# A decoder layer on one core: the turns of x1 and x2 of 13 groups in 32x32 blocks on VectorE and through DRAM, and another order of a round's products

## The reference

```python
x = _layernorm(x + attn(x))            # linear attention: q (k^T v), no softmax
x = _layernorm(x + xattn(x, ctx, mask))# 16 heads of 32, 154 keys, softmax, masked
x = _layernorm(x + ffn(x))             # r = sigmoid(xr Wr); k = relu(xk Wk)^2; out = r * (k Wv)
# xr, xk: mixes of each row with the row before it (mu_r, mu_k)
```

## Time and profile before

| | |
|---|---|
| median of 3 runs | 916.45 us (916.25 to 916.95) |
| the profiled execution | 914.96 us, its span 912.9 us |
| granted TensorE clock | 0.998 of full speed |
| busy share of the span | PE 98%, PEld 82%, DVE 76%, ACT 61%, POOL 57% |
| moved by DMA | 46.54 MB, mean 51 GB/s |

### The profile page before, as it was taken

How to read it: one execution, slowest core, us unless ns; L and a number is a source line. 1 busy time by engine, 2 the same in 40 slices (tenths; PEclk the granted TensorE clock), 3 DMA queues, 4 the chain that set the end, 5 groups by cost and what they waited for, 6 DMA issues and landing times.

```text
span 912.9 us, 23290 instructions
## 1 busy us (share of the span) xinstructions
PE 896.7 (98%) x8774; PEld 749.0 (82%) x8774; DVE 695.6 (76%) x1994; ACT 556.5 (61%) x1667; POOL 521.8 (57%) x505
## 2 busy tenths in 40 slices
PE   8999999999999999999999999999999999999997
PEld 7867766787788888888878888888888888888886
DVE  6688566578877878787877878787877777787775
ACT  7555236858675756575856666666665757575631
POOL 1045015759666666666675757566676767665420
PEclk9999999999999999999999999999999999999999
DMA  8792020113000001012101010101010100100001
GB/s 296 245 271 58 24 94 2 43 36 136 9 25 31 25 25 31 24 32 82 32 24 32 24 32 25 32 25 32 25 32 24 31 26 12 44 2 24 2 24 46
DMA packets 32332, 46.54 MB, mean 51 GB/s; under 512 B 3806, under 2 KB 16606, under 8 KB 32094
## 3 DMA queue, kind: packets, MB, share of 16 engines
q1 hardware_dynamic: 28622, 37.99, 12.8%
q10 hardware_dynamic: 3600, 7.08, 2.3%
HBM read 34.10 MB, written 9.70 MB: 48 GB/s over the span
## 4 chain that ended last, share of the span: by engine, by line
PE 75%; DVE 4%; POOL 4%; issue 4%; ACT 1%; POOLq 0%; ACTq 0%
PE dense L92 19%; PE dense L94 17%; PE dense L93 17%; PE turned L1664 5%; PE turned L1686 5%; PE scores L1650 4%; PE dense L1540 2%; PE turned L1668 1%; PE turned L1540 1%; POOL row_inv L1442 1%; POOL weight L1450 1%; PE scores L1546 1%; DVE mix_k_raw L1204 1%; PE dense L1557 0%; POOL prob_rest L1449 0%
## 5 line engine op out<-in xcount | busy, mean ns | idle before, releaser
L1442 POOL TENSOR_TENSOR row_inv<-row_sum,minus_one 128x4 f32<-128x4 f32 x128 | 152.6, 1192 | 190.1 <-ACT prob L818 190.0
L818 ACT ACTIVATE prob<-prob,row_min 128x154 f32<-128x154 f32 x512 | 209.6, 416 | 39.8 <-DVE row_min L1160 39.8
L1450 POOL TENSOR_TENSOR weight<-prob,row_inv 128x512 f32<-128x512 f32 x128 | 148.0, 1156 | 0.0
L1160 DVE CUSTOM_DVE_ANT_0 prob<-scores,mask_add 128x154 f32<-128x154 f32 x512 | 127.8, 312 | 4.0 <-PE scores L1650 3.7
L826 ACT ACTIVATE prob_t<-turned 128x512 f32<-128x512 f32 x128 | 76.0, 594 | 84.6 <-PE turned L1664 83.8
L818 ACT ACTIVATION_READ_ACCUMULATOR prob<-prob,row_min 128x1 f32 x512 | 98.3, 192 | 0.0
L1664 PE MATMUL turned<-ident,weight 128*128 128x128 f32 x512 | 76.9, 272 | 3.4 <-DVE o_t_lo L1167 3.0
L1664 PEld LDWEIGHTS turned<-ident,weight 128*128 128x128 f32 x512 | 61.2, 139 | 17.9 <-issue 6.3
L92 PE MATMUL dense<-mix_k_hi,ffn_wk_hi 128*128 128x256 f32 x256 | 75.3, 294 | 0.0
L92 PE MATMUL dense<-xt_hi,cross_wq_hi 128*128 128x256 f32 x256 | 75.2, 294 | 0.0
L94 PE MATMUL dense<-mix_k_hi,ffn_wk_lo 128*128 128x256 f32 x256 | 72.3, 283 | 0.0
(11 more groups left out here) (276 smaller groups left out, 2684.7 us busy)
## 6 DMA issues: line engine op xcount, KB each, us to landing
x_rows<-x_rows SPq DMA_DIRECT2D x32, 256.0 KB, 4.6
xt_raw<-x_cols SPq DMA_DIRECT2D x16, 512.0 KB, 3.8
out<-gate_then_y SPq DMA_DIRECT2D x15, 512.0 KB, 2.8
mask_in<-mask SPq DMA_DIRECT2D x16, 154.0 KB, 2.3
cross_wv<-cross_wv SPq DMA_DIRECT2D x2, 512.0 KB, 6.6
cross_wk<-cross_wk SPq DMA_DIRECT2D x1, 1024.0 KB, 9.3
self_wv<-self_wv ACTq DMA_DIRECT2D x1, 1024.0 KB, 7.3
self_wk<-self_wk ACTq DMA_DIRECT2D x1, 1024.0 KB, 9.6
```

The source lines that it names most:

```text
L818: m = act.activation(keys, keys, ACT.Exp, bias=row_min[:, buf, t, h:h + 1], scale=-1.0, accum_out=row_sum[:, buf, t, h:h + 1])
L1160: m = dve.tensor_tensor_reduce(exp_slot(n, u)[:, i * CTX:(i + 1) * CTX], s_bank[:, h, t * CTX:(t + 1) * CTX], mask_add[n % 2][:, t, :], -S ...
L1442: pool.tensor_tensor(row_inv[:, buf, t, :], row_sum[:, buf, t, :], minus_one[:], ALU.pow).then_inc(*p_inv.up)
L1450: pool.tensor_tensor(first, early, inv_early, ALU.mult).then_inc(*p_norm.up)
```

## The change

For the 13 groups 3 to 15 the turn of x1, and for the 13 groups 1 to 13 the turn of x2, is no longer done on PE. VectorE turns each 32x32 block of a tile in place in the grid of blocks (`turn`, one STREAM_TRANSPOSE of 128x512 a tile) into `x1_squares` (over `xt_hi`) or `x2_squares` (over the second half of `o_t_hi` and `o_t_lo`). SP writes that to a DRAM scratch (two transfers of 256 KB a turn) and reads it back so that each block lands on the partitions of its features (four transfers of 128 KB into `xt_raw` for x1, eight of 64 KB into `x_t` for x2). ACT makes the high part of x1 from SBUF in one piece (`x1_high`), DVE the low part (`x1_low`). The rows of a group then stand in blocks of 32, which `spread_product`, `take_q`, `difference` and `blend` follow with access patterns; `difference` becomes two instructions, and the sign of the mix is turned (one small instruction at the start). `x1_high` of a group waits for the fourth transfer back, `o_high(n, 2)` for x2's way out.

The orders of a round on PE, ACT, DVE and POOL are written anew. Core of the diff:

```diff
+            def turn(to, rows, t):
+                return dve.transpose(to[t][:].rearrange("p (j k s) -> p k j s", j=ROWS4, k=KT),
+                                     rows[:, t, :].rearrange("p (k j s) -> p k j s", j=ROWS4, k=KT))
+            def turn_x1(n):
+                dve.wait_ge(*y_mm.at(n))
+                for t in range(TPG):
+                    dve.wait_ge(*ln_ok[1].at(n, t + 1))
+                    turn(x1_squares, x1[n % 2], t).then_inc(*tr1_mm.up)
+            def send_x1(n):
+                for t in range(TPG):
+                    sp.wait_ge(*tr1_mm.at(n, t + 1))
+                    ...
+                    sp.dma_start(x1_park.rearrange("q (j t e) -> q t j e", j=ROWS4, t=TPG)[:, t],
+                                 x1_squares[t][:].rearrange("q (j e) -> q j e", j=ROWS4)).then_inc(*x1_out.up)
+            def fetch_x1(n):
+                sp.wait_ge(*x1_out.at(n - 3))
+                for j in range(ROWS4):
+                    sp.dma_start(x_in[j * SQUARE:(j + 1) * SQUARE, :, :],
+                                 x1_park.rearrange("(i r) (j e) -> j r i e", i=ROWS4, j=ROWS4)[j]).then_inc(*x1_back.up)
+            def x1_high(n):
+                act.wait_ge(*x1_back.at(n - 3))
+                act.activation(xt_hi[:], x_in[:], ACT.Copy).then_inc(*x1t_hi_ok.up)
...
+                if live(f) and moved_x2(f):
+                    send_x2(f)
+                    fetch_x2(f)
+                if live(a) and moved_x1(a):
+                    send_x1(a)
+                    fetch_x1(a)
...
             def v_product(n, t, ks=range(KT)):
                 elif n < LAST - 2:
-                    pe.wait_ge(*q_out.at(n + 3, t + 1))
+                    pe.wait_ge(*r_out.at(n, t + 1))
...
                 transposes(n, 0, 1)
                 o_product(f, 1)
-                y_product(a, 0)
                 values(n, 0)
                 scores(n, 2)
+                y_product(a, 0)
+                transposes(n, 1, 0)
                 y_product(a, 1)
-                transposes(n, 1, 0)
-                r_product(e, 0)
                 transposes(n, 1, 1)
-                r_product(e, 1, early)
-                x2_turn(f, 0)
-                r_product(e, 1, late_half)
-                x1_turn(a, 0)
+                k_product(e, 1)
                 values(n, 1)
                 scores(n, 3)
-                x1_turn(a, 1)
-                x2_turn(f, 1)
-                k_product(e, 1)
+                r_product(e, 0)
                 transposes(n, 2, 0)
+                r_product(e, 1)
+                transposes(n, 2, 1)
+                v_product(e, 0)
+                v_product(e, 1, early)
                 q_product(a, 0)
-                transposes(n, 2, 1)
-                q_product(a, 1)
                 values(n, 2)
                 scores(a, 0)
-                v_product(e, 0)
+                v_product(e, 1, late_half)
                 transposes(n, 3, 0)
-                v_product(e, 1, early)
+                q_product(a, 1, (0,))
                 transposes(n, 3, 1)
-                v_product(e, 1, late_half)
+                q_product(a, 1, (1,))
                 values(n, 3)
                 scores(a, 1)
```

More of the change, by code:

```diff
@@ L598, in main_tiles @@
         tile[f"x2_{i}"] = mem.place(f"x2_{i}", [P, TPG, D])
-    tile["x2t"] = mem.place("x2_t", [P, KT, 1 + GT])
+    tile["x2t"] = mem.place("x2_t", [P, 1 + GT // SQUARE, KT, SQUARE])
+    tile["x2_squares"] = [mem.over(spot, f"x2_squares{i}", [P, D], 4 * D) for i, spot in enumerate(("o_t_hi", "o_t_lo"))]
+    tile["x1_squares"] = [mem.over("xt_hi", f"x1_squares{i}", [P, D], i * 4 * D) for i in range(TPG)]
     tile["gate"] = mem.place("gate_then_y", [P, TPG, D])
@@ L1000, in act_program @@
                 take_rest(n, 3)
-                exponentials(a, 0, 0)
+                take_q(a, 1)
                 exponentials(a, 0, 1)
@@ L1363, in dve_program @@
                     add_one(3)
+            for n in range(2, LAST):
+                a, f, e = n + 1, n - 1, n - 2
+                o_low(f, 3)
+                masked_min(n, 1, 0)
+                masked_min(n, 1, 1)
+                k_square(e, 0)
+                k_low(e, 0)
+                if a == GPB:
+                    next_m_low(2, 3)
+                o_finish(f, 0)
+                o_finish(f, 1)
+                o_low(n, 0)
+                masked_min(n, 2, 0)
+                normalise(2, f, x2[f % 2])
+                turn_x2(f)
+                if n == 2:
+                    weight_low("ffn_wr")
+                y_finish(a, 0)
+                masked_min(n, 2, 1)
+                y_finish(a, 1)
+                normalise(1, a, x1[a % 2])
+                turn_x1(a)
+                k_square(e, 1)
+                o_low(n, 1)
+                masked_min(n, 3, 0)
+                masked_min(n, 3, 1)
+                if n == 2:
+                    weight_low("ffn_wv")
+                k_low(e, 1)
+                make_mask(a)
+                difference(f)
+                x1_low(a)
+                blend(f, "r")
+                v_finish(e, 0)
+                blend(f, "k")
+                carry(f + 1)
+                o_low(n, 2)
+                masked_min(a, 0, 0)
+                masked_min(a, 0, 1)
+                k_mix_low(f)
                 if a == GPB - 1:
                     next_m_low(0, 1)
-                if live(e):
-                    v_finish(e, 0)
-            v_finish(LAST - 3, 1)
+                v_finish(e, 1)
+                normalise(3, e, y3)
             o_low(LAST - 1, 3)
@@ L1540, in turn, with spread_product @@
                     m = pe.transpose(to[:, k * P:(k + 1) * P], rows[:, t, k * P:(k + 1) * P], ident[:])
+                return m
+            def spread_product(to, weight, h, parts):
+                for i in parts:
+                    cols = slice((2 * h + i) * P, (2 * h + i + 1) * P)
+                    for k in range(KT):
+                        m = three_pass(pe, to[:, i * GT:(i + 1) * GT].rearrange("p (b s) -> p b s", s=SQUARE),
+                                       (weight[0][:, k, cols], weight[1][:, k, cols]),
+                                       (moving(xt_hi)[:, k], moving(xt_lo)[:, k]), first=(k == 0), last=(k == KT - 1))
                 return m
```

253 lines of the change are left out of this document (141 added, 112 removed).

## The result

| | before | changed |
|---|---|---|
| median of the runs, us | 916.35 (916.25 to 916.95, 4 runs) | 975.88 (970.77 to 981.96, 4 runs) |
| profiled execution, us | 914.96 | 970.77 |
| its span | 912.9 | 968.6 |
| mean granted clock | 0.998 | 0.974 |
| one round (medians of its products over 13 rounds, added up) | 47.01 | 51.24 |

The account below looks back on a forecast made before the run. PE, busy 47.00 of 47.00 us a round, was taken as the bound. Saving 1.72 less 0.6 lateness leaves 1.12 a round, 14.6 in 13; 914.96 becomes 900.4, plus 1.5 gives 902 us, range 893 to 916.

Parts of the forecast that it names:

- What PE gives up: PE, each round: two turns cost 0.86 us, the four removed 1.72 us, 22.4 us in 13 rounds.
- I cost the reordering itself at nothing: PE's order of products: as many switches between transposes and products as before, so no added time.
- ACT's 3.85 us behind the transfers: ACT from x1's last transfer back to the gate: x1_high, exponentials, take, rest and gate, 3.85 us.
- The walk to v: One round from k_product(e, 0) through DVE, SP and ACT: v due at 32.3 us, its gate done at 32.9.
- I take 2.0: SP, x1's way out to DRAM: 256 KB takes 2.0 us, bounds 2.0 to 2.3.
- At 0.37 to 0.6 they are through before x1's second turn: SP: at that time per issue x2's eight fetches delay nothing; at 0.85 x1 waits another 1.5 us.
- 3.8 for all four together: SP, x1's way back from DRAM: four transfers, 512 KB, 3.8 us in all, bounds 3.1 and 6.4.
- V is late by 0.6 us: PE waits 0.6 us a round for the gate before v, leaving 1.12 of the 1.72 us saved.
- the way round is too long: Rival, x1's way through DRAM: from 1.1 us beyond the walk, lateness eats the 1.72 saved; 923 or 935 us; chance 0.15.
- q's strided operand: Rival on PE: q's 48 matmuls, reading runs of 32 columns, take half more, 2.9 us a round, 938 us; chance 0.05.
- DVE isn't the bound: Judges the rival that DVE, 40 busy of 45.3 us, becomes the bound: 0.5 us a round more, 908; chance 0.05.
- The wrong name: Sign on PE: a wait of q for xt_lo or y for x, not v for the gate, would show a misnamed wait.

Follow-up runs that it names:

- the last experiment: Against the kernel before: only x2 turned on VectorE and sent through DRAM, x1 left on TensorE, VectorE and ACT work reordered; 907.53 us, ratio 0.9901.
- the sixth experiment: Changed kernel with x1_high behind the gate, x1's transfers ahead of x2's on SP, and DVE and ACT work reordered to suit; 946.65 us, ratio 1.0346 to the kernel before.

## Why the prediction was wrong, point by point

- **What PE gives up: right.** 0.86 for two turns, shown by the last experiment for x2's; x1's stand at the same price by estimate.
- **"I cost the reordering itself at nothing": wrong by 0.6 us a round**, as an estimate from the starts of products. With the round trip cut, v's remaining wait of 0.7 comes on top, and the round was 46.64. I counted switches between transposes and products, not which product stands where.
- **DVE's turn at 0.69: right** (0.69, two take 1.30). ACT's 3.85 us behind the transfers: right; from 508.84 to the gate's end 512.75 are 3.9.
- **The walk to v, term by term.** Means of 13 rounds in the changed kernel's trace, us, 0 being the start of `k_product(e, 0)`:

| | predicted | measured |
|---|---|---|
| x1's second turn ends | 23.3 | 24.2 (median 23.8) |
| from there to the first fetch | 2.0 | 3.8 |
| from there to `x1_high` | 3.8 | 4.3 |
| from there to v | 3.85 | 4.1 |
| v is due | 32.3 | 32.5 (median 32.2) |
| v is late | 0.6 | 3.9, of which PE stood idle 3.7 |

- **"I take 2.0" for the way out: the term that was sized worst.** It was the `out` row. In the five rounds in which nothing stood ahead of them, x1's two sends took 2.9 to 3.6 from the last turn to the first fetch, outside the bounds of 2.0 to 2.3; waiting for x2's fetches adds 0.7 on average. Why the two `out` transfers of the earlier trace rows were quicker was not tested: they ran alone at the end of the kernel, and in longer runs (2048 bytes each, where x1's sends have 512).
- **"At 0.37 to 0.6 they are through before x1's second turn": true in seven of 13 rounds, by a hair.** Eight fetches took 3.66 us (0.46 each) in eight rounds and up to 4.89 in the others, and x2's way out took 2.9 to 4.8 for 2.0. In those five rounds in which x1's first send left at once, v still waited 2.9 to 3.3 us: the queue behind x2 made the lateness longer, it didn't make it.
- **"3.8 for all four together": 4.3.** Near, and inside the bounds.
- These give the failed step, **"V is late by 0.6 us"**: 3.7 were measured. Of the 3.2 us more, 2.4 are the way through DRAM (8.2 for 5.8: 1.1 the way out itself, 0.7 the queue, 0.5 the way back), 0.6 are DVE's walk up to x1's turns against PE's own, 0.2 ACT's work behind the transfers.
- **"The clock" stood in no term: 1.67 us a round missing.** The trace of before had nothing at half clock in the loop, so it gave no row for it. The filled gap shows that it is a price of its own.
- **The rival "the way round is too long" is what happened**, by its mechanism and past its break-even of 1.1 us; its 935 came from issues of 0.85 us, which took 0.43 to 0.61, and lacked the clock and the order. I gave it 0.15. "For it" stood the right fact, one queue with 16 more transfers; I weighed it by issue time and not by landing time.
- **The other rivals:** q's strided operand costs nothing (q's matmuls start 0.122 us apart, before 0.120). DVE isn't the bound: a round from 489.90 to 540.10 has it busy 36.0 of 50.2 us. The wrong name would have been a wait for `xt_lo`; it appeared only once the gate's and v_finish's were out of the way (20.2 us in the run with only the first step of v_finish moved).

Not tried: x1 alone in the order before, and x1's own transfers on another queue than SP's.

## What to carry to other kernels

Where the bound engine is saturated, moving work to another one is worth exactly its own time, but only if its consumer is further away than the whole detour; measure that distance in the trace first (x2 had 14.4 us, and its way took 9.5 to 11.2; x1's way took 8.2, and by the walk its copy was due 5.2 after its turns, 32.3 - 3.85 - 23.3) and move only the pieces that have it. The engine that takes the work over must have room at that place too: with x2 alone in the old order the way was hidden, and a round still became 0.38 us longer. The order can give a consumer more room, as it did for x1 in the sixth experiment, but there the new order cost more than the turns gave. Price a transfer through DRAM as send + landing + issues + landing, each several times over if the queue is shared, never by the fastest lone transfer. And after each swap read the name of the wait again: in an in-order queue, what stands behind a late piece is late too, even if it has nothing to do with it.

## What the runs showed of the hardware

- With idle stretches of PE of 2.9 to 5.0 us came 3.4 us or 6.8 us at granted clock 0.50, in 12 of 13 rounds. With the gap partly filled with matmuls that compute nothing needed, the half clock fell from 53.6 to 17.3 us and the kernel became 14 us faster. The Trainium skill ("TensorE: Matmul & The Clock Gate", section "What's actually happening") says that the clock halves after idleness and comes back under load; by that, the trace agrees: 1.00 ahead of the idle stretch, 0.50 behind it, and 1.00 again from 518.1 on, with PE at work.
- An issue on SP took 0.60 us for a send of 256 KB and 0.43 for each of x1's four fetches. x2's eight took 3.66 us together in eight of 13 rounds (0.46 each) and up to 4.89 in the others (0.61 each); in the kernels with x2 alone 3.66 in most rounds, at most 4.62. 512 KB out and back took 7.7 to 8.4 us from the first send to `x1_high` (7.7 from 501.12 to 508.84).
- The same DVE instruction can take quite different times. Two rows of the kernel with x2 alone, reordered:

```profile
532.53 2.55 DVE L1245 SCALAR_TENSOR_TENSOR mix_k_raw<-mix_r_raw,cols,x_t 128x256 f32<-128x256 f32 x4
...
538.21 1.22 DVE L1251 TENSOR_TENSOR mix_k_lo<-mix_k_raw,mix_k_hi 128x1024 fp32r<-128x1024 f32 x1
```

The four blends for k took 2.55 us in eight of the twelve rounds from 260 us on, some 1.87 in the other four, and 1.78 in most rounds of the kernel before. The low part took 1.22, with POOL idle until 539.33, and 2.06 in the kernel before, with POOL busy in 70% of that time. But POOL at work is not enough to explain it: it was busy in 98% of the stretch in which the kernel before did its four blends in 1.78. The cause was not tested. Where a row varies so, its mean is no price.
